# A reciprocal from a table seed and two Newton steps in the first layer of a fused two-layer kernel

## The reference, cut to what matters

```python
xn = layernorm(x)
xm = xn * time_mix + shift(xn) * (1 - time_mix)
k, v, r = xm @ Wk.T, xm @ Wv.T, xm @ Wr.T        # k, v with time last
k = exp(minimum(k, 60.0)); kv = k * v
wkv = causal_depthwise_conv(kv, w)               # w decays with distance: a scan
wk  = causal_depthwise_conv(k, w) + 1e-9
s   = (sigmoid(r) * (wkv / wk)) @ Wo.T
g   = silu(three +-1 dense layers of xn)         # 128 -> 512 -> 512 -> 128
x   = x + s * g
```

## Time and profile before

| | us |
|---|---|
| three runs: median (lowest to highest) | 673.99 (672.09 to 675.5) |
| the profiled execution: its own time | 672.1 |
| its span | 670.3 |
| first layer, body 3 begins on PE (its `turn_rows`) | 57.20 |
| body 15 begins on PE | 243.47 |
| first matmul of the second layer | 271.14 |

### The profile page before, as it was taken

One profiled execution on the slowest core, in us unless ns is written; L12 is line 12 of the kernel. 1 busy time (PEld: TensorE's weight loads), 2 busy tenths in 40 slices (PEclk: granted clock), 3 DMA queues, 4 the chain that ended last, 5 costly groups with the idle time before them and its releaser, 6 DMA issues. The chain is left out here.

```text
span 670.3 us, 9285 instructions
## 1 busy us (share of the span) xinstructions
PE 629.5 (94%) x2714; PEld 304.2 (45%) x2714; DVE 601.0 (90%) x1406; ACT 511.4 (76%) x794; POOL 280.1 (42%) x275
## 2 busy tenths in 40 slices
PE   4779999999999998799999999999999999999986
PEld 2334444444444443344545444454444544444442
DVE  4999999999999999988988988898898899889856
ACT  2846666666666665889988898898888889899886
POOL 6556777777777765222123032122313303221220
PEclk9999999999999999999999999999999999999999
DMA  7331000000000000000000000000000000000000
GB/s 178 109 94 31 1 0 1 1 0 1 0 2 1 0 1 1 1 0 1 16 1 17 17 4 14 16 17 0 17 17 1 17 17 17 0 18 17 0 17 32
DMA packets 10770, 11.65 MB, mean 17 GB/s; under 512 B 4800, under 2 KB 6288, under 8 KB 10720
## 3 DMA queue, kind: packets, MB, share of 16 engines
q1 hardware_dynamic: 9744, 10.73, 5.3%
q0 software_dynamic: 112, 0.33, 0.1%
q10 hardware_dynamic: 864, 0.00, 0.1%
HBM read 6.87 MB, written 4.19 MB: 16 GB/s over the span
## 5 line engine op out<-in xcount | busy, mean ns | idle before, releaser
L1150 PE MATMUL bank<-arena,w 128*128 128x512 f16 x640 | 148.6, 379 | 4.1 <-DVE arena L774 4.1
L1150 PE MATMUL bank<-arena,dnT 128*128 128x512 f32 x288 | 138.6, 592 | 0.0
L435 POOL TENSOR_TENSOR arena<-arena 128x512 f32<-128x512 f32 x48 | 59.7, 1271 | 137.6 <-ACT arena L590 137.6
L650 ACT ACTIVATE arena<-bank,xinv 128x512 f32<-128x512 f32 x144 | 94.4, 693 | 24.9 <-PE bank L1150 24.6
L1150 PEld LDWEIGHTS bank<-arena,w 128*128 128x128 f16 x640 | 62.5, 98 | 78.3 <-issue 10.1
L482 ACT ACTIVATE arena<-bank 128x512 f16<-128x512 f32 x96 | 53.8, 606 | 35.8 <-PE bank L1150 35.8
L425 POOL TENSOR_TENSOR arena<-arena 128x512 f32<-128x512 f32 x16 | 16.8, 1050 | 140.6 <-DVE arena L1011 140.6
L1150 PEld LDWEIGHTS bank<-arena,dnT 128*128 128x128 f32 x288 | 53.7, 191 | 35.9 <-issue 24.4
L1150 PE MATMUL bank<-arena,wsqT 128*128 128x512 f32 x128 | 64.6, 609 | 5.3 <-DVE arena L783 5.3
L1020 DVE SCALAR_TENSOR_TENSOR arena<-bank,cws,arena 128x506 f32<-128x506 f32 (+1 forms) x96 | 67.1, 740 | 1.1
L774 DVE SCALAR_TENSOR_TENSOR arena<-bank,arena 128x512 f16<-128x512 f32 x96 | 60.3, 671 | 2.4 <-ACT arena L482 1.2
(11 more groups left out here) (221 smaller groups left out, 1492.6 us busy)
## 6 DMA issues: line engine op xcount, KB each, us to landing
x_all<-in_L_attn_x SPq DMA_DIRECT2D x16, 256.0 KB, 2.6
out<-x_all SPq DMA_DIRECT2D x16, 256.0 KB, 2.0
up_n<-in_L_ffn_routed_up SPq DMA_DIRECT2D x1, 512.0 KB, 3.7
dn_n<-in_L_ffn_routed_down SPq DMA_DIRECT2D x1, 512.0 KB, 5.3
wx<-in_L_attn_W_x SPq DMA_DIRECT2D x1, 288.0 KB, 2.9
k_u<-in_L_ffn_k POOLq DMA_DIRECT2D x1, 256.0 KB, 5.8
w_in<-in_L_attn_W_in SPq DMA_DIRECT2D x1, 256.0 KB, 2.7
k_u<-in_L_ffn_k SPq DMA_DIRECT2D x1, 128.0 KB, 6.1
```

The costliest lines, as they stand in the source:

```text
L435: g.tensor_tensor(prod[:, c, :], act[:, c + 1, :], gate[:, :], ALU.mult).then_inc(sem["b_actp"], 1)
L650: a.activation(act[:, c, :], up_bank(f, c)[:, :], ACT.Gelu, scale=xinv[:, I_UP:I_UP + 1]).then_inc(sem["b_act"], 1)
L1150: return nc.tensor.matmul(ps, lhsT, rhs, start=start, stop=stop)
```

## The change

The reciprocal of `wk` is no longer taken by VectorE's RECIPROCAL in two halves. ScalarE makes a rough one: `wk`'s bits read as an integer, times a constant, plus `seedb`, through Exp. VectorE then does two Newton steps on the whole tile: `ya = wk * rec`, `rec = (ya - 2.00045) * rec`, `ya = wk * rec`, and last `ya = (ya + 2) * ysr`, where GpSimd has meanwhile put `ysr * rec` into `ysr`. So `ya`, once made by GpSimd, is now made by VectorE, and its sign is turned by `c3[:, 3:4]` in `sg`. GpSimd's product no longer waits for the end of the reciprocal but for the first Newton step, and `wk` of the next group waits for `ya`. The scan of kv goes behind the four `low` of layer 0 and behind `gp`; `turn_back` goes behind `hidden1(m, 1)`.

```diff
 # GpSimd, layer0
-                    pool.wait_ge(sem["a_rec"], m + 1)
+                if has(m):
+                    pool.wait_ge(sem["a_r1"], m + 1)
                     pool.wait_ge(sem["a_ysr"], m + 1)
-                    after(pool, sem["a_s"], m)
-                    g.tensor_tensor(ya[:, :], ysr[:, :], rec[:, :], ALU.mult).then_inc(sem["a_y"], 1)
+                    g.tensor_tensor(ysr[:, :], ysr[:, :], rec[:, :], ALU.mult).then_inc(sem["a_q"], 1)
...
                 if has(f):
+                    after(pool, sem["a_y"], f)
                     pool.wait_ge(sem["a_wkc"], f + 1)
 # ScalarE, layer0, ahead of high(1, m, 0); the same in last_hidden
+                if has(m):
+                    actv.wait_ge(sem["a_wk"], m + 1)
+                    after(actv, sem["a_q"], m)
+                    a.activation(rec[:, :], wk[:, :].bitcast(mybir.dt.int32), ACT.Exp, scale=SEED_SCALE,
+                                 bias=seedb[:, :]).then_inc(sem["a_rec"], 1)
 # VectorE
+            def first_product(n):
+                dve.wait_ge(sem["a_rec"], n + 1)
+                after(dve, sem["a_s"], n)
+                v.tensor_tensor(ya[:, :], wk[:, :], rec[:, :], ALU.mult).then_inc(sem["a_t1"], 1)
+            def first_step(n):
+                dve.wait_ge(sem["a_t1"], n + 1)
+                v.scalar_tensor_tensor(rec[:, :], ya[:, :], NEWTON, rec[:, :], ALU.subtract, ALU.mult).then_inc(sem["a_r1"], 1)
+            def second_product(n):
+                dve.wait_ge(sem["a_r1"], n + 1)
+                v.tensor_tensor(ya[:, :], wk[:, :], rec[:, :], ALU.mult).then_inc(sem["a_t2"], 1)
+            def second_step(n):
+                dve.wait_ge(sem["a_t2"], n + 1)
+                dve.wait_ge(sem["a_q"], n + 1)
+                v.scalar_tensor_tensor(ya[:, :], ya[:, :], 2.0, ysr[:, :], ALU.add, ALU.mult).then_inc(sem["a_y"], 1)
 # VectorE, layer0
                 if has(m):
-                    dve.wait_ge(sem["a_wk"], m + 1)
-                    after(dve, sem["a_y"], m)
-                    v.reciprocal(rec[:, 0:N // 2], wk[:, 0:N // 2])
+                    first_product(m)
+                    first_step(m)
+                    second_product(m)
...
+                if has(m):
+                    second_step(m)
...
-                    v.reciprocal(rec[:, N // 2:], wk[:, N // 2:]).then_inc(sem["a_rec"], 1)
                     low(1, m, 2)
                     low(1, m, 3)
...
-                    v.scalar_tensor_tensor(sg[:, :], b_S[:, :], c3[:, 2:3], gp[:, :], ALU.mult, ALU.mult).then_inc(sem["a_sg"], 1)
+                    v.scalar_tensor_tensor(sg[:, :], b_S[:, :], c3[:, 3:4], gp[:, :], ALU.mult, ALU.mult).then_inc(sem["a_sg"], 1)
 # VectorE, last_hidden
-                v.reciprocal(rec[:, 0:N // 2], wk[:, 0:N // 2])
+                first_product(m)
+                first_step(m)
                 normalised(0, "b_")
+                second_product(m)
...
-                v.reciprocal(rec[:, N // 2:], wk[:, N // 2:]).then_inc(sem["a_rec"], 1)
                 low(1, m, 2)
                 turned_low(0)
+                second_step(m)
                 low(1, m, 3)
 # TensorE, layer0
+                if has(m):
+                    hidden1(m, 1)
                 if has(t):
...
                     turn_back(b_RX).then_inc(sem["a_sgT"], 1)
-                if has(m):
-                    hidden1(m, 1)
```

More of the change, by code:

```diff
@@ L18 @@
 WK_EPS = 1e-9
+LOG2 = math.log(2.0)
+SEED_SCALE = -LOG2 / 2 ** 23
+SEED_BIAS = LOG2 * (127 - 0.043)
+NEWTON = 2.00045
 K_CAP = 60.0
@@ L30 @@
 a_stat a_vareps a_rstd a_centred a_xn a_xnT a_prev a_xh a_xm a_xl a_k a_v a_r a_ek a_ekm a_kv a_scanK a_scanV
-a_wkc a_kvc a_wk a_wkv a_thr a_sr a_ysr a_rec a_y a_z0 a_z1 a_hi0 a_hi1 a_lo0 a_relu a_low a_lo1 a_s a_f a_thf a_gp a_sg a_sgT a_x1
+a_wkc a_kvc a_wk a_wkv a_thr a_sr a_ysr a_rec a_t1 a_r1 a_q a_t2 a_y a_z0 a_z1 a_hi0 a_hi1 a_lo0 a_relu a_low a_lo1 a_s a_f a_thf a_gp a_sg a_sgT a_x1
 b_stat b_vareps b_rstd b_centred b_xn b_xnT b_xh b_xl b_xin b_res b_rout b_u0 b_conv b_xc b_xch b_xcl b_r
@@ L84, in build @@
         epsc = sb("epsc", [P, J])
+        seedb = sb("seedb", [P, 1])
         wsq = sb("wsq", [P, 4, P])
@@ L382, in _ @@
             g.memset(s2B[:, :], 0.0).then_inc(sem["rank_clear"], 1)
+            g.memset(seedb[:, :], SEED_BIAS)
             g.memset(ones[:, :], 1.0).then_inc(sem["const_ready"], 1)
@@ L562, in last_hidden @@
             def last_hidden():
+                m = G - 1
+                actv.wait_ge(sem["a_wk"], m + 1)
+                actv.wait_ge(sem["a_q"], m)
+                a.activation(rec[:, :], wk[:, :].bitcast(mybir.dt.int32), ACT.Exp, scale=SEED_SCALE,
+                             bias=seedb[:, :]).then_inc(sem["a_rec"], 1)
                 high(1, G - 1, 0)
@@ L767, in decays @@
                 v.tensor_scalar(c3[:, 2:3], c3[:, 1:2], 0.5, None, ALU.mult)
+                v.tensor_scalar(c3[:, 3:4], c3[:, 1:2], -0.5, None, ALU.mult)
                 v.tensor_scalar(dec[:, 0:P], ones[:, :], tch[:, 1:2], None, ALU.mult)
                 v.tensor_scalar(dec[:, P:T], ones[:, 0:T - P], tch[:, 1:2], None, ALU.mult).then_inc(sem["const_done"], 1)
+            def first_product(n):
[12 more added lines that the diff above has]
+                v.scalar_tensor_tensor(ya[:, :], ya[:, :], 2.0, ysr[:, :], ALU.add, ALU.mult).then_inc(sem["a_y"], 1)
             def low(layer, n, j):
@@ L831, in layer0 @@
                     largest()
[L832 to L838, removed]
                 if has(f) and f != 0:
@@ L847, in layer0 @@
                     v.scalar_tensor_tensor(gp[:, :], thf[:, :], 1.0, b_F[:, :], ALU.add, ALU.mult).then_inc(sem["a_gp"], 1)
+                if has(f):
+                    dve.wait_ge(sem["a_kv"], f + 1)
+                    after(dve, sem["a_wkv"], f)
+                    for s in range(SEQ):
+                        last = v.tensor_tensor_scan(Pv[:, s, 1:], dec[:, :], kv[:, s * T:(s + 1) * T], 0.0,
+                                                    ALU.mult, ALU.add)
+                    last.then_inc(sem["a_scanV"], 1)
+                if has(m):
                     dve.wait_ge(sem["a_gp"], m + 1)
```

2 lines of the change are left out of this document (removed).

## The result

The changed kernel takes 694.78 us (median of 4 runs, 693.5 to 695.52), the kernel before 673.95 beside it: a ratio of 1.0308, 95% interval 1.0278 to 1.0339. That is slower, by 20.8 us. The forecast was 687.5, its range 677 to 692. The direction holds, and so does the mechanism in the twelve equal bodies. The size is 7 us off and outside the range. The changed kernel's profiled execution took 695.0 against 672.1, 22.9 more; its span is 692.8, 22.5 more. Executions of one kernel differ by several us with TensorE's mean granted clock: the kernel before, run again beside the experiments, took 671.15 at 1.00 and 675.86 at 0.992.

A forecast was written before the change was run, and what follows sets the result against it. The prediction saw a loop through VectorE, GpSimd, TensorE and ScalarE as the bound, then VectorE. Equal bodies +11.4, bodies 1 and 2 0, crossing +2.2 made +13.6 on 672.1, 685.7; with the median 1.9 higher, 687.5 us, range 677 to 692.

The forecast's parts named there:

- Bodies 1 and 2 ... gain as much by shorter instructions as they lose: 0.: First layer's early bodies, with scales and maxima: no net change, between -0.6 and +1 us.
- The body before, 15.54: Kernel before, 12 equal first-layer bodies: 186.47 us in all, 15.54 us each.
- Undisturbed VectorE's body, 13.98: VectorE's time per equal body after the change, without interference from GpSimd: 13.98 us.
- Exclusion, in all its four places: GpSimd's full tiles delay first product, first step, `ekm` and scans of k: 0.40, 0.77, 0.46, 0.81 us a body.
- Its floor, put at 14.9: TensorE's own least time per equal body, from its busy 179.0 us over 12 bodies: 14.9 us.
- The body, 16.47: Equal first-layer body after the change: 16.47 us, +0.95 each, +11.4 us over 12 bodies.
- The walk: Step-by-step timing of VectorE and GpSimd through one equal body from `xm`'s start: 2.44 us lost, body 16.42 us.
- The crossing, +2.2: Passage from first to second layer: `xn` copies interleaved with GpSimd's tiles, +2.2 us, between +1 and +3.
- The clock: Open point: TensorE's granted clock might fall during its waits of 1.3 us a body.
- rival 3: Worse order at the ties, or a falling clock while TensorE waits: +0.3 us a body, 692 us; chance 0.08.
- Rival 1: Products and steps not excluded, or falling between GpSimd's tiles; TensorE's 14.9 us a body rules, 666 us; chance 0.12.
- rival 2: Only TENSOR_TENSOR and scans excluded, first step saves 0.77 us, body 15.7, total 677 us; chance 0.10.

The follow-up runs named there:

- psum4: Changed kernel with all four Newton instructions in the first layer's bodies taking one operand from PSUM, values meaningless: 672.05 us, ratio 0.9988.
- low_between_start: Kernel before, RECIPROCAL kept, layer-0 `low` between scans of kv and k, later `turn_back`, early k scans in bodies 0 and 1, idle matmuls in body 2: 666.22 us.
- scan_early_body1: Changed kernel with the scan of kv back at its old place in bodies 0 and 1 only: 691.41 us, ratio 1.0279.
- order_only: Kernel before, RECIPROCAL kept, with only the new places of the scan of kv and `turn_back`: 678.48 us, ratio 1.0074.
- fill_body2: Changed kernel with 16 idle matmuls on TensorE before body 2's k product: 693.02 us, ratio 1.0295.
- newton_spread: Changed kernel's arithmetic, VectorE's order in bodies 2 to 15 chosen to avoid GpSimd's tiles, with old kv place in bodies 0 and 1 and body-2 idle matmuls: 674.34 us.

## Why the prediction was wrong in size

The step that failed is the pricing of the odd bodies: "Bodies 1 and 2 ... gain as much by shorter instructions as they lose: 0." They lost 4.5 us. Next comes the size of the loss in the equal bodies, 3.1 us too small. The cause it named for those bodies was right. Term by term:

- **The body before, 15.54.** The window of the earlier trace rows begins at 57.00, body 3 at 57.20, so that 186.47 holds 0.2 too much; 186.27 / 12 = 15.52, which is what the sums use.
- **Undisturbed VectorE's body, 13.98.** Right: 14.00 by the rows, with 0.69 and 0.68 for the second product and step.
- **Exclusion, in all its four places.** Right. Predicted losses 0.40, 0.77, 0.46 and 0.81, measured 0.58, 0.84, 0.48 and 0.83; the second product, `kv` and the second step free, as forecast. psum4 shows the cause for the four Newton instructions by taking it away. For `ekm` and the scans it is shown by their place: 0.41 and 1.26 in low_between_start, where they meet no tile.
- **TensorE** waits 1.36 a body, for `low` alone; some 1.3 were forecast, the larger part before `hidden1`, where it is 0.76. Its floor, put at 14.9, is lower: low_between_start has bodies of 14.70 with TensorE's work unchanged.
- **The body, 16.47.** Mis-sized: 16.73. The term is twelve times 0.95 = 11.4, and measured twelve times 1.21 = 14.5, 3.1 more. The walk let `wkv` start 0.07 after the scan of kv (ending at -0.60 by its clock), and it starts 0.15 after (the scan ends at 181.19, GpSimd starts at 181.34 in the next body); everything behind it on GpSimd comes later by that. The first `hl` ends 3.23 after `xm`'s start, not 3.07, the first product 3.78, not 3.61, the first step 5.34, not 5.10. The four losses are larger than forecast by 0.18, 0.07, 0.02 and 0.02, which is the 0.29 between 2.73 and 2.44. That the later `wkv` is the reason is read from the traces; no run moved it alone.
- **"Bodies 1 and 2 ... gain as much by shorter instructions as they lose: 0."** This is the step that failed. They lost 3.37 + 1.12 = 4.5 us: 1.64 in body 1's own instructions, with the first step, `ekm` and the scans of k held by GpSimd's tiles, 1.73 in the chain of scales, and 1.12 in body 2, of which 0.93 are the clock. The term named the scales, but priced none of their meetings with GpSimd's tiles; its own upper bound was +1. The moved scan of kv was counted "nothing by itself, but it makes `wkv` and `ysr` 3 us later on GpSimd"; these 3 us put them, and the two `hl`, onto the chain. The trace of scan_early_body1 gives back 2.95 of the 4.5; order_only has the longer chain without any Newton step. The 1.04 ahead of body 1 was in no term, and is not shown to belong to the change.
- **The crossing, +2.2.** The number is right, +2.33, but by luck. The four copies of `xn` take 3.77 where they took 2.13, interleaved with two `hl` and the product, as forecast:

```profile
285.48 3.77 DVE L756 TENSOR_SCALAR xn<-x_all,mv,rstd 128x128 f32<-128x128 f32 x4
```

  But other work there became shorter: body 15 takes 15.61 from `xm` to its row statistics where it took 16.16, which no term had. Most of the +2.33 is TensorE's clock, which was not in this term either. In the changed kernel, then in fill_body2, whose code is the same here:

```profile
289.31 0.72 PE L1203 MATMUL bank<-ident,xn 128*128 128x128 f32 x4 [3.32 <-DVE xn L756]
289.82 3.55 PE L1192 MATMUL bank<-arena,w 128*128 128x512 f16 x8
```

```profile
288.49 0.66 PE L1203 MATMUL bank<-ident,xn 128*128 128x128 f32 x4 [3.31 <-DVE xn L756]
288.99 1.89 PE L1192 MATMUL bank<-arena,w 128*128 128x512 f16 x8
```

  The granted clock is 0.53 from 289.8 to 293.4 in the first and 1.00 in the second. In fill_body2 the stretch from `xm` of body 15 to the second layer takes 26.41, only 0.64 more than before: 1.69 of the 2.33 are the clock.
- **The clock.** In rival 3 as an open point, for waits of 1.3 us: at those it stays at 1.00 from body 3 to body 15. It fell at places that the prediction did not name: behind the wait of 4.24 us in body 2 and behind that of 3.32 at the crossing. The length of the wait does not decide it alone: at the crossing the eight matmuls take 3.04 behind 2.01 us in order_only, and 1.89 behind 2.60 in newton_spread and behind 3.31 in fill_body2. What does is open.
- **Rival 3** priced a body 0.3 above the forecast, and 0.26 was measured, but not by its mechanism: GpSimd's product does not go ahead of the second product, which takes 0.69.
- **Rival 1** falls with the 1.27 of L793, **rival 2** with the 1.53 of L798: the form with two SBUF inputs of SCALAR_TENSOR_TENSOR is excluded like TENSOR_TENSOR. The Trainium skill's rule (SBUF — State Buffer, Who interferes with whom), which speaks of two SBUF inputs in general and names neither this form nor the scan, holds for both here: 1.53 against 0.69, and 2.09 against 1.26.
- Together: 13.6 forecast, 3.1 in the equal bodies, 5.5 ahead of them and 0.1 at the crossing are 22.3 of the 22.4 between the two profiled executions. Two of these places differ between kernels with the same code there: by 0.67 ahead of body 1 (24.99 in psum4, 25.66 in the changed kernel) and by 1.69 at the crossing. So one profiled execution of each kernel can't settle the last 2 us. Against the medians the forecast of +13.6 missed 7.2 of the 20.8.

## What to carry to other kernels

Before you exchange one long VectorE instruction for several short ones, ask what GpSimd does at that time. In this case RECIPROCAL and work with an operand in PSUM lay beside its tiles for nothing. Work with two operands in SBUF did not (psum4: 672.05 against 694.78 us), and neither did a TENSOR_SCALAR from SBUF to SBUF (`ekm`, 0.90 against 0.42). Then either feed one operand from PSUM, or place the contested instructions by GpSimd's timeline, and check the order anew for each arithmetic. Price the odd bodies of a pipeline, first, second and last, by their own rows: the moved instruction meets other work there. And compare a term that you find right with a second kernel whose code is the same at that place, as fill_body2 at the crossing.

## What the runs showed of the hardware beyond this

- The exclusion doesn't ask how small the VectorE instruction is: in the changed kernel a TENSOR_TENSOR of 128x1 took 1.22 us and a TENSOR_SCALAR of 128x7 0.93 and 1.00 behind GpSimd's tiles, against 0.16 for the same three in scan_early_body1, where they meet none. The chain of small instructions lost 1.73 us, more than any full tile of a body (0.84).
- ScalarE's Exp with its input in SBUF read as int32 takes 0.72, the Exp from PSUM in f32 0.60 (both of the changed kernel). The type need not be the reason: L534, which reads f32 from SBUF with a factor for each channel, takes 0.72 as well, and the seed has such an operand in `seedb`. No run separates the two.

```profile
163.09 0.72 ACT L515 ACTIVATE arena<-arena,seedb 128x512 f32<-128x512 int32 x1
167.74 0.60 ACT L523 ACTIVATE arena<-bank 128x512 f32<-128x512 f32 x1
```
